# Attention block with the score matmuls moved ahead of the transposes and projection pieces in each slot

## Time and profile before

| | |
|---|---|
| time, median of 3 runs | 3923.45 us (3922.22 to 3924.38) |
| the profiled execution: time, span | 3922.59 us, 3920.8 us |
| busy: TensorE, its weight loads | 3823.5 us (98%), 3143.7 us (80%) |
| busy: ScalarE, VectorE, GpSimd | 3022.9 us (77%), 2663.7 us (68%), 1991.4 us (51%) |
| chain that ended last | TensorE 90%, VectorE 4%, ScalarE 3% |
| granted TensorE clock, mean | 0.998 of full speed |

### The profile page before, as it was taken

How to read it: one execution, slowest core, us unless ns; L and a number is a source line. 1 busy time by engine, 2 the same in 40 slices (tenths; PEclk the granted TensorE clock), 3 DMA queues, 4 the chain that set the end, 5 groups by cost and what they waited for, 6 DMA issues and landing times.

```text
span 3920.8 us, 97172 instructions
## 1 busy us (share of the span) xinstructions
PE 3823.5 (98%) x39180; PEld 3143.7 (80%) x39180; DVE 2663.7 (68%) x4379; ACT 3022.9 (77%) x5141; POOL 1991.4 (51%) x1030
## 2 busy tenths in 40 slices
PE   6999999999999999999999999999999999999998
PEld 5878788787888878888787888878878788787886
DVE  5776666666676676666666676676766666666665
ACT  5887877878777787777877788787887877878776
POOL 2454544545445464454644546455454544545444
PEclk9999999999999999999999999999999999999999
DMA  2011111111112121121111211112111110111111
GB/s 89 20 51 48 53 47 26 55 42 55 47 26 58 36 58 44 26 66 31 55 47 26 68 28 53 47 34 65 26 53 47 43 57 23 52 47 47 47 26 52
DMA packets 100722, 178.49 MB, mean 46 GB/s; under 512 B 16192, under 2 KB 16192, under 8 KB 100288
## 3 DMA queue, kind: packets, MB, share of 16 engines
q1 hardware_dynamic: 100288, 172.29, 15.7%
HBM read 71.57 MB, written 33.55 MB: 27 GB/s over the span
## 4 chain that ended last, share of the span: by engine, by line
PE 90%; DVE 4%; ACT 3%; issue 2%; DMA 0%; POOL 0%; SPq 0%; ACTq 0%; DVEq 0%
PE psum L494 36%; PE psum L513 13%; PE psum L544 11%; PE psum L546 11%; PE psum L566 6%; PE psum L570 6%; PE psum L568 6%; DVE max_parts L730 1%; PE psum L503 1%; ACT p_hi L644 1%; ACT p_full L643 1%; PE psum L521 1%; DVE q_shift L716 1%; ACT q_hi_hi L626 1%; DVE p_lo L749 0%
## 5 line engine op out<-in xcount | busy, mean ns | idle before, releaser
L410 POOL TENSOR_TENSOR p_lo<-p_full,p_hi 128x1024 f16<-128x1024 f32 x768 | 1646.1, 2144 | 1746.4 <-ACT p_hi L644 1745.4
L643 ACT ACTIVATE p_full<-psum,prob_bias 128x512 f32<-128x512 f32 x2048 | 1427.9, 697 | 672.0 <-PE psum L546 664.8
L730 DVE TENSOR_REDUCE max_parts<-psum 128x1 f32<-128x512 f32 x2048 | 1379.8, 687 | 737.0 <-PE psum L513 729.9
L644 ACT ACTIVATE p_hi<-psum,prob_bias 128x512 f16<-128x512 f32 x2048 | 1424.1, 695 | 0.0
L566 PEld LDWEIGHTS psum<-v_parts,p_hi 128*128 128x128 f16 x8192 | 744.5, 98 | 243.6 <-issue 153.9
L513 PE MATMUL psum<-k_lo_hi,q_hi_hi 128*128 128x512 f32 x2048 | 848.0, 435 | 25.2 <-issue 22.2
L566 PE MATMUL psum<-v_parts,p_hi 128*128 128x65 f16 x8192 | 858.8, 193 | 5.3 <-ACT p_hi L644 2.7
L568 PE MATMUL psum<-v_parts,p_hi 128*128 128x64 f16 x8192 | 852.7, 192 | 0.0
L570 PE MATMUL psum<-v_parts,p_lo 128*128 128x65 f16 x8192 | 850.2, 194 | 0.0
L544 PE MATMUL psum<-q_hi_hi,k_lo_hi 128*128 128x512 f32 x2048 | 806.0, 394 | 11.8 <-ACT p_hi L644 8.1
L546 PE MATMUL psum<-q_shift,k_shift 128*128 128x512 f32 x2048 | 801.9, 392 | 0.0
(11 more groups left out here) (59 smaller groups left out, 4721.8 us busy)
## 6 DMA issues: line engine op xcount, KB each, us to landing
x_in<-in_xT SPq DMA_DIRECT2D x128, 256.0 KB, 3.0
q_hi_hi<-q_hi_hi SPq DMA_DIRECT2D x256, 128.0 KB, 2.2
k_shift<-k_lo_hi SPq DMA_DIRECT2D x256, 128.0 KB, 2.3
y_tile<-in_x SPq DMA_DIRECT2D x128, 256.0 KB, 2.7
result<-y_tile SPq DMA_DIRECT2D x128, 256.0 KB, 2.0
o_heads<-in_L_conv_w_qkv SPq DMA_DIRECT2D x12, 256.0 KB, 4.1
o_heads<-in_L_conv_w_out SPq DMA_DIRECT2D x4, 256.0 KB, 4.9
out_bias<-in_L_conv_b_out SPq DMA_DIRECT2D x1, 256.0 KB, 4.3
```

Of the source, the lines that this page charges most:

```text
L410: nc.gpsimd.tensor_tensor(p_lo[:, g % LO_SLOTS, :, :], p_full[:, g % 2, :, :], p_hi[:, g % HI_SLOTS, :, :], ALU.subtract).then_inc(p_lo_re ...
L643: nc.scalar.activation(p_full[:, g % 2, n, :], scores(g, n), ACT.Exp, scale=SCALE, bias=prob_bias[:, :])
L644: nc.scalar.activation(p_hi[:, g % HI_SLOTS, n, :], scores(g, n), ACT.Exp, scale=SCALE, bias=prob_bias[:, :]).then_inc(exp_done, 1)
L730: nc.vector.reduce_max(max_parts[:, u % 2, q_tile, k_half:k_half + 1], bank(b, w), AX.X).then_inc(done["row_max"], 1)
```

## The change

In each slot TensorE's call of `step_scores(g + 1)` moves from behind the fills to ahead of the transposes. The orders of all other engines, the bank plan, the semaphores and their counts stay as they are.

```diff
                 for b in batches:
                     for w in ring_early(g - STEPS * b):
                         ring(b, w)
+                if is_step(g + 1):
+                    step_scores(g + 1)
                 for b in batches:
                     for w in transposes_of_slot(g - STEPS * b):
                         transpose(b, w)
                 for b in batches:
                     for piece in fills_of_slot(g - STEPS * b):
                         fill(b, *piece)
-                if is_step(g + 1):
-                    step_scores(g + 1)
                 for b in batches:
                     for w in ring_late(g - STEPS * b):
                         ring(b, w)
```

## The result

The changed kernel takes 3974.49 us (median of 4 runs, 3973.70 to 3975.09) against 3923.06 for the kernel before on the same footing: a ratio of 1.0131, with a 95% interval of 1.0113 to 1.0148. It is slower by 51 us; the forecast was 3968, by 45.

A forecast was written before the change was run, and what follows sets the result against it. TensorE, busy 98% of the span, was taken as the bound, so reordering only adds or removes its waits: 3922.6 us + 69.2 of losses - 24 of gains = 3968 us, range 3930 to 3990 (likeliest case alone 3950 to 3983).

The forecast's parts named there:

- Loss 1, V pieces: 16 V slots a batch: ScalarE's v_hi delays the next exp, so the second score tile waits; 46.4 us lost.
- The 0.14 of a V slot: Lateness in us of the second score tile after an ordinary V piece, as in slots 11, 15 and 23.
- Loss 2, the shift row: Slots 35 and 51: scores wait for VectorE's shift row, no longer covered by the projection piece; 0.45 each, 14.4 us.
- Loss 3, slot 48: Scores in slot 48 wait longer for ScalarE's exp, 1.36 instead of 0.80; 8.4 us lost.
- Gains: Earlier releases for fills and transposes in slots 0 (10.5 us), 3, 4, 6, 8 (9.6) and 62 (about 4): 24 us.
- its 0.16: How early in us a release must precede its matmul: 0.05 wait plus 0.11 late weight load.
- Cheap late releases: Rival: weight loads are pulled ahead past waits, so each new wait costs 0.11 less; 26 us less, 3942; chance 0.14.
- Every shift row late: Rival: ten more slots a batch pay 0.1 each for the shift row, 16 us more, 3984; chance 0.09.
- the ten slots that came to live on 0.01: Slots where the shift row needs 1.15 and the scores are due at 1.16 after the change.
- Faster by the Q/K chain: Rival: ScalarE's earlier hi part removes the waits of slots 34, 42, 50 and the shift-row loss; 3908; chance 0.09.
- Nothing: Rival: ScalarE's lead swallows most of the V-piece loss and the sum closes near 0; 3923; chance 0.08.

The follow-up runs named there:

- run 1: Changed kernel with ScalarE's v_hi one place later, behind the first exp tile of the next slot: 3922.02 us, 0.9996 of the kernel before.
- run 2: Changed kernel with scores put back behind the fill in the 16 slots with a V piece: 3917.31 us, 0.9983 of the kernel before.
- run 5: Changed kernel with ScalarE making the high part of each V piece twice, first into a spare buffer: 4034.97 us, 1.0276 of the kernel before.
- run 3: Changed kernel with scores put back behind the fill in slots 35, 48 and 51 alone: 3944.16 us, 1.0052 of the kernel before.
- run 4: Kernel before the change, with the new order only in slots 62, 63 and 0 to 8: 3905.83 us, 0.9955 of the kernel before.
- run 7: Changed kernel with VectorE taking the Q/K low parts first in slots 34, 42 and 50: 4019.90 us, 1.0237 of the kernel before.

## Why the prediction was right

**The balance.** 45 us were forecast and 51 measured. By the table, losses are 79 us (forecast 69.2) and gains some 32 (forecast 24). Both were sized too small, by 10 and by 8 us, and that the sum is off by only 6 is in part luck. The spans differ by 51.8, 4 more than the table gives. Of these, 1.6 lie ahead of the first step (61.1 against 59.5 us from the start), where the traces of the other runs go from 59.2 to 61.3; that is scatter. Another 1.6 are a single wait in slot 51 of the sixth batch, in the changed kernel's trace:

```profile
1460.33 0.62 ACT L600 CAST xT_hi<-x_in 128x512 fp32r<-128x512 f32 x1 [1.57 <-DMA x_in<-in_xT]
...
1462.16 0.50 PE L544 MATMUL psum<-q_hi_hi,k_lo_hi 128*128 128x512 f32 x1 [1.37 <-ACT p_hi L644]
```

ScalarE waited 1.57 for a load of X that came late, the exps behind it were late, and S with them. The prediction had put the DMAs at nothing. In the trace of the kernel before, S waits behind no late load.

**Loss 1, V pieces.** 1.20 × 16 + 2.00 × 15 = 49 us, forecast 46.4. Runs 1 and 2 take it away from either side, and run 5 shows the slope: 0.27 us more in v_hi is 0.27 us more wait, 60 us in all as worked out. The 0.14 of a V slot was 0.15.

**Loss 2, the shift row.** 0.46 in each of two slots, forecast 0.45; shown by run 3.

**Loss 3, slot 48.** 0.59, forecast 0.56. But run 3 showed that it is not a loss of S alone: with the old order the wait comes back behind S.

**Gains.** Slot 0 gave 0.91 × 15 = 14 us for 10.5; I had kept 0.17 of the wait, and nearly nothing stayed. The additions' slots (3, 4, 6, 8) gave 9.7 for 9.6, slot 62 the 4 us. Shown by run 4. The 9.6 was right by luck, though. The prediction split its 0.16 into a wait of 0.05 and a late load of 0.11. By starts F came 0.14 late, and the late load gave back only 0.02: behind transposes the matmul after F's first takes 0.31 instead of 0.23 in the changed kernel too. Left out of the sum, but there: 0.06 each in slots 19, 27 and 43, and 0.07 in 50, together 4 us.

**What was missed.** Slots 2, 11, 20 and 28: 0.1 each a batch, 6 us, none of it in the sum. The release comes just before the matmul is due but after its weights would have loaded. So it is in slot 20 of the ninth batch, where the exp ends at 2085.41:

```profile
2084.69 0.72 ACT L644 ACTIVATE p_hi<-psum,prob_bias 128x512 f16<-128x512 f32 x1
...
2085.48 0.49 PE L544 MATMUL psum<-q_hi_hi,k_lo_hi 128*128 128x512 f32 x1
2085.81 0.39 PE L546 MATMUL psum<-q_shift,k_shift 128*128 128x512 f32 x1
```

What the prediction called free is another thing, the V pieces made in slots 20, 28 and 60, whose wait would fall on the S of slots 21, 29 and 61; these three did stay free. The S of slots 20 and 28 pay for the V pieces of 18 and 26: slots 19 and 27 have no F, so ScalarE is still behind one slot later, and run 1 takes this away with the rest.

**The rivals.** *Cheap late releases:* refuted; each new wait carries the 0.11, as in 2057.37 to 2057.71 above. The weight load did not pass the wait. The Trainium skill ("TensorE: Matmul & The Clock Gate", section "Architectural detail: the array is 16× 32×32, not 1× 128×128") says that TensorE's queue can pull weight loads ahead of matmuls in flight. The traces agree for a free stream, where the load runs ahead (2028.63 for the matmul of 2028.86 in run 1), and show that it stops at a wait (2057.37 above). *Every shift row late:* of the ten slots that came to live on 0.01 only slot 11 pays, 0.09. *Faster by the Q/K chain:* the changed kernel's waits in 34, 42 and 50 are 0.97, 0.96 and 0.96 a batch against 0.97, 0.96 and 1.03, so the earlier hi part freed nothing, and VectorE's order is the releaser in the dead heat. Run 7 shows both halves: the hi part is indeed ready earlier, and using it first only moves the delay into the shift. *Nothing:* refuted by the result.

## What to carry to other kernels

Where TensorE is full, price a reorder by writing down, for each wait of its next few slots, when the releasing queue gets there and when TensorE does; here margins of a tenth of a microsecond repeated from batch to batch almost without scatter and were worth a forecast. Moving a producer behind a consumer takes cover away from the chains that hang on the producer, here v_hi: look at what the in-order engine has *behind* the op that waits, and move that op one place down before giving up the reorder. An order that pays in some slots and costs in others can be chosen by slot: run 4 keeps nearly the gains alone.

## What the runs showed of the hardware that was not expected

A release that comes just ahead of its matmul still costs 0.1 us. In the changed kernel's middle batches, where the exp ended 0.06 or 0.07 us ahead of the second score tile, that tile started on time and the matmul behind it came 0.33 later; where it ended 0.19 us or more ahead, 0.23. The matmul's own line shows no idle time for this, only that of its weight load does, and a late release shows up for the most part as TensorE's busy time (3857.0 against 3823.5 us for the same work).

Waits of TensorE of about 2 us, once in each of three slots a batch, were followed by a granted clock of 0.50 in 12 of 48 cases (run 7, mean 0.994). In the changed kernel (mean 0.998) the steady waits are 1.3 us at most, and the clock did not fall behind them, nor behind the single one of 1.5 us. Why it fell behind some waits of run 7 and not behind others is open.
